# Signalling TensorE's edge products once per four steps, with a ring of eight steps in the relations stage

## What is computed

```python
def _L0_gnn_ref(h, weight, norm, src, dst, rel_type):
    transformed = jnp.einsum('ni,rio->rno', h, weight)
    msg = transformed[rel_type, src] * norm
    return jax.ops.segment_sum(msg, dst, num_segments=h.shape[0])

def gat_conv(x, src, dst, W, a_src, a_dst, b):      # twice, with elu between
    h = (x @ W).reshape(N, HEADS, HEAD_DIM)
    e = leaky_relu(alpha_s[src] + alpha_d[dst])
    ex = jnp.exp(e - segment_max(e, dst)[dst])
    alpha = ex / (segment_sum(ex, dst)[dst] + 1e-16)
    return segment_sum(h[src] * alpha[:, :, None], dst).reshape(N, 256) + b
```

## Time and profile before

| | |
|---|---|
| median of three runs | 3737.38 us |
| the profiled execution's own time | 3720.8 us |
| its span | 3719.0 us, 38781 instructions |
| busy: PE, PE weight load, DVE | 2090.7, 1652.9, 1597.0 us |
| busy: POOL, ACT | 1512.9, 939.0 us |
| mean granted TensorE clock | 0.732 |

### The profile page before, as it was taken

One profiled execution on the slowest core, in us unless ns is written; L12 is line 12 of the kernel. 1 busy time (PEld: TensorE's weight loads), 2 busy tenths in 40 slices (PEclk: granted clock), 3 DMA queues, 4 the chain that ended last, 5 costly groups with the idle time before them and its releaser, 6 DMA issues.

```text
span 3719.0 us, 38781 instructions
## 1 busy us (share of the span) xinstructions
PE 2090.7 (56%) x12121; PEld 1652.9 (44%) x12121; DVE 1597.0 (43%) x4904; ACT 939.0 (25%) x2022; POOL 1512.9 (41%) x1544
## 2 busy tenths in 40 slices
PE   6698655656617888641444444455144444444599
PEld 5587433333417887631333333344133333333377
DVE  3100333333434444441555555576155555555834
ACT  4243000000003333231233322233133222233212
POOL 1000666666440000145555555523555555553223
PEclk9899566666559999865777776677566666667679
DMA  5244333333337888633333333321333333332000
GB/s 183 116 192 186 109 110 110 110 111 102 88 114 234 281 270 281 201 120 87 93 93 92 96 103 92 93 65 64 90 92 92 93 93 92 93 93 83 1 12 24
DMA packets 210393, 432.86 MB, mean 116 GB/s; under 512 B 34916, under 2 KB 117389, under 8 KB 203725
## 3 DMA queue, kind: packets, MB, share of 16 engines
q0 software_dynamic: 69280, 195.96, 19.0%
q1 hardware_dynamic: 131548, 225.86, 17.6%
q10 hardware_dynamic: 9360, 8.52, 0.7%
HBM read 343.69 MB, written 87.33 MB: 116 GB/s over the span
## 4 chain that ended last, share of the span: by engine, by line
PE 31%; issue 30%; DVE 12%; POOL 10%; DMA 7%; another core or an unknown queue 7%; DVEq 1%; SPq 1%; ACT 1%; POOLq 0%; ACTq 0%
POOL arena L672 9%; PE banks L397 8%; DMA arena<-in_L_ffn_w_dram 5%; PE banks L1016 4%; PE banks L1326 3%; PE banks L1327 3%; PE banks L1294 2%; PE banks L1313 2%; DVE arena L1456 2%; DVE arena L1491 2%; PE banks L1028 1%; SPq L977 1%; DVE arena L1410 1%; DMA arena<-tr,idx1T 1%
## 5 line engine op out<-in xcount | busy, mean ns | idle before, releaser
L1219 POOL DMA_INDIRECT arena<-ht,srcT x884 | 865.9, 979 | 815.5 <-PE banks L1327 530.0
L672 POOL DMA_INDIRECT arena<-tr,idx1T x442 | 422.8, 957 | 426.0 <-DMA tr<-arena 224.7
L1313 PE MATMUL banks<-arena 128*128 128x8 bf16 (+1 forms) x2688 | 83.4, 169 | 791.6 <-issue 791.5
L1313 PEld LDWEIGHTS banks<-arena 128*128 128x128 bf16 x2688 | 78.1, 104 | 798.5 <-issue 798.5
L1326 PE MATMUL banks<-arena,XT 128*128 128x264 f32 x884 | 355.2, 491 | 90.4 <-DVE arena L1410 69.7
L683 PE MATMUL banks<-arena 128*128 128x256 f32 x442 | 231.9, 623 | 250.7 <-issue 139.4
L1327 PE MATMUL banks<-arena,XT 128*128 128x264 f32 x884 | 331.1, 463 | 0.0
L1491 DVE TENSOR_TENSOR arena<-arena,nrmT 128x528 f32<-128x528 f32 x448 | 311.4, 701 | 21.2 <-ACT nrmT L1272 20.4
L397 PE MATMUL banks<-parts 128*128 128x512 f32 x1200 | 281.0, 397 | 49.9 <-DVE parts L425 49.9
L1016 PE MATMUL banks<-arena 128*128 128x128 f32 x2080 | 258.8, 284 | 65.4 <-DMA arena<-in_L_ffn_w_dram 65.2
L1016 PEld LDWEIGHTS banks<-arena 128*128 128x128 f32 x2080 | 247.4, 198 | 78.8 <-DMA arena<-in_L_ffn_w_dram 78.2
(11 more groups left out here) (303 smaller groups left out, 3463.9 us busy)
## 6 DMA issues: line engine op xcount, KB each, us to landing
arena<-in_L_ffn_w_dram SPq DMA_DIRECT2D x195, 512.0 KB
tr<-arena SPq DMA_DIRECT2D x50, 1024.0 KB, 3.9
XT<-dld SPq DMA_DIRECT2D x56, 512.0 KB
arena<-ht,srcT POOLq DMA_INDIRECT x884
xg<-arena SPq DMA_DIRECT2D x13, 640.0 KB
arena<-xg SPq DMA_DIRECT2D x65, 128.0 KB
yg<-arena ACTq DMA_DIRECT2D x65, 128.0 KB, 4.9
arena<-tr,idx1T POOLq DMA_INDIRECT x442
```

Of the source, the lines that this page charges most:

```text
L672: pool.indirect_dma_start(Gr[:, n, h, :], None, TR, bass.IndirectOffsetOnAxis(ap=idx1T[:, q:q + 1], axis=0)).then_inc(d_g[n], 16)
L1219: pool.indirect_dma_start(G[c % NG4][:, j, :], None, HT[L], bass.IndirectOffsetOnAxis(ap=srcT[:, q:q + 1], axis=0)).then_inc(d_gat[c % NG4 ...
L1313: mm = ten.matmul(B[6][:, n:n + m], OHb[b][:, j, :], SB[:, j, o:o + m], start=(j % 2 == 0 and i == 0), stop=(j % 2 == 1 and i == 2))
```

## The change

PE raises `gm_ok` on the last step of every group of `GS` = 4 steps (and on the last step of all), and `pr_ok` on the last step of each half chunk. Whoever waits for a step now waits for the count of its group. In relations the ring is eight steps and DVE makes masks seven steps ahead of the adds, and the buffers are laid out anew. In attention POOL waits at the first and the ninth gather of a chunk for the half chunk four back, where it waited at every fourth gather for two more steps. The threshold in `dve_combine` only follows the ring's size. The diff:

```diff
@@ -37,8 +37,9 @@
 MT = (2 * NP + R * (P - 1)) // P
 GT = 5
 NGR = NT // GT
-NG = 6
-LAG = 3
+NG = 8
+LAG = 7
+GS = 4
 NW = 3
 HALF = 15
 
@@ -651,11 +652,13 @@
 
         top[0] = base0
         Gr = take(NG * 2 * D).rearrange("p (n a d) -> p n a d", n=NG, a=2)
+        OHr = take(NG * 2 * P).rearrange("p (n a d) -> p n a d", n=NG, a=2)
+        top[0] = max(top[0], 16384)
         zer = take(D)
-        OHr = take(NG * 2 * P).rearrange("p (n a d) -> p n a d", n=NG, a=2)
         xf = X[:, :, :].rearrange("p t d -> p (t d)")
         xo = Offsets(vec, rv, D, (NS - 1) * D)
         d_g = sems("d_g", NG)
+
         d_zg, oh_r, gm_ok, ga_ok = (sem(n) for n in ("d_zg", "oh_r", "gm_ok", "ga_ok"))
 
         def pool_gather():
@@ -666,7 +669,7 @@
             for s in range(SU):
                 n = s % NG
                 if s >= NG:
-                    pool.wait_ge(gm_ok, s - NG + 1)
+                    pool.wait_ge(gm_ok, (s - NG) // GS + 1)
                 for h in range(2):
                     q = 2 * s + h
                     pool.indirect_dma_start(Gr[:, n, h, :], None, TR,
@@ -681,7 +684,9 @@
                 if s >= NG:
                     ten.wait_ge(ga_ok, s - NG + 1)
                 ten.matmul(B[n][:, 0:D], OHr[:, n, 0, :], Gr[:, n, 0, :], start=True, stop=False)
-                ten.matmul(B[n][:, 0:D], OHr[:, n, 1, :], Gr[:, n, 1, :], start=False, stop=True).then_inc(gm_ok, 1)
+                mm = ten.matmul(B[n][:, 0:D], OHr[:, n, 1, :], Gr[:, n, 1, :], start=False, stop=True)
+                if s % GS == GS - 1 or s == SU - 1:
+                    mm.then_inc(gm_ok, 1)
 
         def dve_gather():
             vec.wait_ge(tm_ok, 8 * NT)
@@ -691,7 +696,7 @@
                 if s < SU:
                     n = s % NG
                     if s >= NG:
-                        vec.wait_ge(gm_ok, s - NG + 1)
+                        vec.wait_ge(gm_ok, (s - NG) // GS + 1)
                     for h in range(2):
                         q = 2 * s + h
                         vec.tensor_scalar(OHr[:, n, h, :], iorow[:, :], dlT[:, q:q + 1], nrmT[:, q:q + 1], ALU.is_equal,
@@ -704,13 +709,13 @@
                         vec.wait_ge(ga_ok, q)
                     o = xf[:, bass.ds(xo.at(q), D)]
                     ins = vec.tensor_tensor(o, o, B[q % NG][:, 0:D], ALU.add)
-                    ins.wait_op(gm_ok, q + 1, "sem-ge")
+                    ins.wait_op(gm_ok, q // GS + 1, "sem-ge")
                     ins.then_inc(ga_ok, 1)
 
         def sp_gather():
             sync.wait_ge(k_ok, ZEROS)
             for k in range(MT // 5):
-                sync.wait_ge(gm_ok, 13 * k + 13)
+                sync.wait_ge(gm_ok, (13 * k + 12) // GS + 1)
                 sync.dma_start(XG[k * 5 * P:(k * 5 + 5) * P, :].rearrange("(t p) d -> p t d", p=P),
                                zer.rearrange("p (o d) -> p o d", o=1).to_broadcast([P, 5, D])).then_inc(d_zg, 16)
 
@@ -1112,7 +1117,7 @@
 
         def dve_combine(g):
             for i in range(g * GT, g * GT + GT):
-                vec.wait_ge(d_g[i % 4], 32 * 37 + 32 * (i // 4 + 1))
+                vec.wait_ge(d_g[i % 4], 32 * ((SU + NG - 4) // NG) + 32 * (i // 4 + 1))
                 step(vec.scalar_tensor_tensor(X[:, i, :], YB[i % 4][:, 0, :], m8[:, i, 0:1], X[:, i, :], ALU.mult, ALU.add))
                 vec.scalar_tensor_tensor(X[:, i, :], YB[i % 4][:, 1, :], m8[:, i, 1:2], X[:, i, :], ALU.mult,
                                          ALU.add).then_inc(cb_ok, 1)
@@ -1213,8 +1218,8 @@
                 pool.wait_ge(d_ht[b], 16 * (L + 1) * (7, 6, 6, 6)[b])
             for c in range(NCH):
                 for j in range(2 * steps_of(c)):
-                    if c >= NG4 and j % 4 == 0:
-                        pool.wait_ge(pr_ok, SU * L + (c - NG4) * CH + j // 2 + 2)
+                    if c >= NG4 and j % 8 == 0:
+                        pool.wait_ge(pr_ok, 2 * (L * NCH + c - NG4) + j // 8 + 1)
                     q = c * CC + j
                     pool.indirect_dma_start(G[c % NG4][:, j, :], None, HT[L],
                                             bass.IndirectOffsetOnAxis(ap=srcT[:, q:q + 1], axis=0)).then_inc(d_gat[c % NG4], 16)
@@ -1255,7 +1260,7 @@
                 b, k = c % 2, L * NCH + c
                 act.wait_ge(ob_ok, k + 1)
                 if c > 1:
-                    act.wait_ge(pr_ok, SU * L + CH * (c - 1))
+                    act.wait_ge(pr_ok, 2 * (L * NCH + c - 1))
                 act.copy(OH[b], OHb[b]).then_inc(oh_ok, 1)
 
             masks(0)
@@ -1324,8 +1329,9 @@
                     if c * CH + j > 3:
                         ten.wait_ge(ad_ok, t - 3)
                     ten.matmul(B[n][:, 0:MSG], OH[b][:, 2 * j, :], G[c % NG4][:, 2 * j, 0:MSG], start=True, stop=False)
-                    ten.matmul(B[n][:, 0:MSG], OH[b][:, 2 * j + 1, :], G[c % NG4][:, 2 * j + 1, 0:MSG], start=False,
-                               stop=True).then_inc(pr_ok, 1)
+                    mm = ten.matmul(B[n][:, 0:MSG], OH[b][:, 2 * j + 1, :], G[c % NG4][:, 2 * j + 1, 0:MSG], start=False,
+                                    stop=True)
+                mm.then_inc(pr_ok, 1)
 
             for i in range(-2, NCH):
                 c, n, q = i, i + 1, i + 2
@@ -1408,7 +1414,7 @@
                         vec.wait_ge(dv.sem, state["rescaled"])
                     o = ACC[:, bass.ds(ao_.at(c * CH + j), MSG)]
                     ins = vec.tensor_tensor(o, o, B[j % 4][:, 0:MSG], ALU.add)
-                    ins.wait_op(pr_ok, t + 1, "sem-ge")
+                    ins.wait_op(pr_ok, 2 * (L * NCH + c) + j // 4 + 1, "sem-ge")
                     ins.then_inc(ad_ok, 1)
                     yield
```

## The result

The changed kernel takes 3796.51 us (median of 4 runs, 3787.53 to 3801.55); the kernel before took 3735.15 beside it (3730.85 to 3737.91). The ratio is 1.0159, 95% interval 1.0139 to 1.0178: slower, where 3687 us was forecast. The profiled execution of after is its slowest run, 3801.55 us, span 3799.8 (before 3720.8 and 3719.0).

The account below looks back on a forecast made before the run. Bound: attention's loop of gather burst, late `e_ok` and products. From the profiled 3720.8 us, -72 (burst), +14 (VectorE), +8 (relations) give 3670.8, plus 16.6 to the median: 3687 us; own range 3640 to 3725.

Parts of the forecast that it names:

- What bounds the kernel: Attention: TensorE's completions arrive late during gathers; burst, `e_ok` and products hold each other back in a loop of 30.75 us.
- Increments at nothing: TensorE's signals, relations and attention: 495 fewer increments taken to save 0 us; the skill's 26.3 ns each would save 13 us.
- POOL's wait: Start of an attention chunk: POOL waits for product 3, not 1, so the burst starts 2.4 us later on 48 chunks.
- What the later burst gives back: Attention: fewer TensorE instructions behind the burst's start bring `e_ok` earlier; net -1.5 us a chunk, -72 us, best chunk 28.7.
- VectorE in attention: Adds waiting for their group's last product: hidden where gathers run, 1.7 us in each of eight chunks without, +14 us.
- Relations: Ring of eight and masks seven ahead: one limit goes, one of the same size comes; +8 us, bounds -78 and +45.
- the first: Rival, attention: `e_ok` goes on arriving only 2.4 us after a burst's end; slower, 3874 us, chance 0.30.
- The second: Rival: increments are what is served late, so `e_ok` comes on time; much faster, about 3340 us, chance 0.07.
- the third: Rival, a wash: gain and delay cancel in each attention chunk, relations gives a little back; 3738 us, chance 0.11.

Follow-up runs that it names:

- e5: Kernel before, POOL's burst gated on the maxima of chunk c-2 and all products of chunk c-4; 3570.8 us against 3723.5, ratio 0.9597, chip 3.
- e3: Changed kernel with every step signalling again, relations too, every wait at the same product as in the changed kernel; 3138.8 us, 1.0077 of before, chip 15.
- e8: Same kernel as e3, on chip 5: every step signals, waits as in the changed kernel; 3141.7 us against 3115.5 before, ratio 1.0079.
- e11: Same kernel as e3, again on chip 15: every step signals, waits as in the changed kernel; 3139.4 us against 3114.7 before, ratio 1.0075.
- e14: Same kernel as e3, once more on chip 15: every step signals, waits as in the changed kernel; 3137.9 us against 3117.0 before, ratio 1.0065.
- e2: Kernel before with the attention part of the diff alone, relations as before; 3140.4 us against 3115.2, ratio 1.0077, chip 15.
- e7: Changed kernel with every attention product signalling and each VectorE add waiting for its own product; 3691.6 us against 3723.5 before, ratio 0.9930, chip 3.
- e0_before: The kernel before itself, unchanged, run for a profile on chip 3; 3741.1 us, one run.
- e9: Kernel before with one wait changed: VectorE's attention adds wait for products 3 and 7, not their own; 3139.3 us against 3115.5, ratio 1.0077, chip 5.
- e10: Changed kernel with one more signal a chunk, on product 1, behind which POOL starts as before; 3138.1 us against 3115.5 before, ratio 1.0073, chip 5.
- e1: Kernel before with the relations part of the diff alone, attention as before; 3116.2 us against 3115.2, ratio 1.0003, chip 15.

## Why the prediction was wrong

*What bounds the kernel* held on a late chip: the loop of burst, `e_ok` and products. e5 shortened it at the place read from the earlier trace rows: 4.0 us less from `e_ok` to the next burst, of which 3.4 a chunk arrived, since the burst itself grew by 0.8.

*Increments at nothing*: nothing was seen on chips 5 and 15 (e3, e8, e11 and e14 against e2). The 26.3 ns for each that the Trainium skill gives (TensorE: Matmul & The Clock Gate, "The cost: per-tile semaphore tail") would have put e3, with 330 more signals in attention than e2, some 9 us above it, an estimate from that page; they are level at 1.0077. With intervals of 0.3% to either side, near 9 us, this speaks against the page's figure here and doesn't exclude it. On a late chip the step is untested.

*POOL's wait, +2.4 us a chunk*: right where `e_ok` stays late. Those chunks went from 30.71 to 32.88, +2.2.

*What the later burst gives back, -1.5 us, best chunk 28.7*: the mechanism was right and the size was too large. e7, with the later burst and own adds, has 43 of 46 `e_ok` inside the burst, 19 chunks are under 29 us, the shortest 28.1, and the mean fell by 1.15 us against e0_before. That is 53 us over the periods where 72 had been forecast, and in the medians e7 is 32 us under before where the whole sum had -50. That its 3691.6 lies near the forecast's 3687 is luck: chip 3 started from 3723 and not from 3737. The two lengths in the earlier trace rows already held the floor: signals behind `e_ok` are late too, so an early `e_ok` is passed on only in part. In the changed kernel itself this term and the next together measured +56 us over the 46 periods of the first measurement, not -72.

*VectorE in attention, +14 us, hidden where gathers run*: **this step failed, as far as the runs tell.** I looked at whether the two instructions queued between the adds end before `e_ok` comes, saw that they do, and took the adds' wait at nothing in the 46 periods with gathers; but an `e_ok` that comes late for want of something else isn't a cover that stays put. Between e7 and the changed kernel on chip 3, that is, own adds and six more signals a chunk against held adds, `e_ok` moved from 13.7 to 19.0 us after the burst's start, only 31 of 46 stayed inside it, and the chunks inside lengthened from 29.24 to 30.13. Over the 46 that is 71 us (1426 less 1355) where the forecast had 0; the medians are 62 apart. That it is the adds is argued and not shown: on chip 5 their wait alone cost +0.8% (e9) and the number of signals changed nothing (e8 against e10, e3 against e2 on chip 15), but on a late chip the two were not taken apart. Where I had priced the wait, in the eight chunks without gathers, it was 0.6 to 0.8 us in each of the last periods of a layer and not 1.7: some 6 of 14 us.

With these figures chip 3 adds up: -53 for the burst, +71, +6, +1.5 for relations and +3 in the first four chunks of the two layers give +29 us; the medians are 30 apart. The first measurement, +61, doesn't: there only 27 of 46 `e_ok` came inside the burst and those chunks took 30.82. Some 30 us of it stay open.

*Relations, +8 us*: +3.5 on the first chip (995.24 to 998.77), +1.5 on chip 3 (994.6 to 996.1), nothing to be seen on chip 15 (e1). POOL's idle, 77.8 and 76.5 us, fits the argument that one limit went and one of the same size came; no run took the two apart.

*The rivals*: the first (`e_ok` only behind the burst, 3874 us) has the right sign, and 19 of the 46 periods are as it says, 2.2 us longer where it had 2.4; in the other 27 `e_ok` did move inside, so it is 77 us too high. The second falls, the third was within 60 us. None named the adds.

## What to carry to other kernels

When waits are coarsened, price each consumer's wait by itself, and undo it by itself: here the producer's fewer signals and POOL's later start cost nothing that was seen on chips 5 and 15, and the one consumer that handed buffers back step by step cost all that was lost there. On a late chip the adds were not taken apart from the signals. A wait that "is hidden because another signal is later" must be checked against what makes that other signal late. And where a burst of one engine holds up signals of another, start the burst behind the last signal that the chain needs (e5: -4.0% where it matters, level elsewhere), not behind the first buffer that comes free.

## What the runs showed of the hardware

The same kernel takes 3735 us on the chip of the first measurement, 3723 on chip 3, and 3115 on chips 5 and 15, a factor of 1.2, with medians from 3114.7 to 3117.0 on the latter. Between the profiles of before and of e1 all but some 8 of 612 us lie in the stages where POOL gathers. On the late chips matmuls of 0.17 us leave 0.7 or 1.4 us apart while gathers are being issued, and the signal of `expand` comes up to 16 us behind the recorded end of the instruction, at distances from the burst's start that go in steps of 0.7 us; on chip 15 (e1) 48 of them take 1.36 us beside the same gathers and POOL never waits for a product. The mean granted clock was 0.72 to 0.75 on the late chips and 0.77 to 0.80 on the others, but that doesn't explain it: the 48 matmuls of the maxima take 1.42 us in the median chunk of before and of e9 alike. Why one chip does this and another doesn't, no run shows.

A gather of 0.95 us takes 1.14 us on average beside line 1491 of e9 (a VectorE multiply of 128x528 out of SBUF) and 0.95 beside line 1410 (an add of 128x264 that reads a PSUM bank). So a POOL that waits for nobody can still be slowed by where VectorE's work lies: 14.5 us in e9.
